# Routed expert stage: the scatter-add issued one tile later, four output buffers, expert weights split in pieces

## The reference

```python
x = x + L0_ffn(L0_cond(x, itok_B_1_198, cond0), ...)      # layer 0: dense FFN with top-2 LoRA experts
x = x + L1_ffn(L1_cond(x, itok_B_0_7, cond1, side), ...)  # layer 1: top-2 of 8 experts, and a shared one

# L1_ffn: t = 2048 tokens, d = 512, E = 8 experts, h = 352, K = 2
scores = softmax(x @ gate_w);  topk_w, topk_idx = top_k(scores, K)
comb = zeros((T, E)).at[arange(T)[:, None], topk_idx].add(topk_w)
g = silu(einsum('td,edh->teh', x, w_gate)) * einsum('td,edh->teh', x, w_up)
routed = einsum('teh,ehd,te->td', g, w_down, comb)
shared = silu(x @ sw_gate) * (x @ sw_up) @ sw_down
out = routed + shared
```

## Time and profile before

| | |
|---|---|
| median of 3 runs | 1144.67 us (1143.12 to 1146.67) |
| profiled execution | 1144.04 us, its span 1142.4 us |
| mean granted TensorE clock | 0.973 of full speed |
| TensorE matmuls busy | 1054.6 us, 92% |
| VectorE, ScalarE, GpSimd busy | 45%, 26%, 37% |
| GpSimd busy, 850 to 900 us | 38.99 of 50 us |
| chain that ended last: TensorE, VectorE, GpSimd, DMA | 76%, 7%, 5%, 5% |
| scatter-add, 39 of them | 1.60 us issue (median), 5.0 us to landing |
| gather, 39 of them | 1.00 us issue (median), 3.4 us to landing |

### The profile page before, as it was taken

One profiled execution on the slowest core, in us unless ns is written; L12 is line 12 of the kernel. 1 busy time (PEld: TensorE's weight loads), 2 busy tenths in 40 slices (PEclk: granted clock), 3 DMA queues, 4 the chain that ended last, 5 costly groups with the idle time before them and its releaser, 6 DMA issues.

```text
span 1142.4 us, 15264 instructions
## 1 busy us (share of the span) xinstructions
PE 1054.6 (92%) x4995; PEld 864.2 (76%) x4996; DVE 518.5 (45%) x776; ACT 299.0 (26%) x522; POOL 418.2 (37%) x403
## 2 busy tenths in 40 slices
PE   7847999999999999999979999999988889999995
PEld 4636888788878888788847777778777878889894
DVE  3395666644464445644475324362533224331400
ACT  1531222111111111111131110210034434444442
POOL 3663334440000000000025000027178778888984
PEclk9967999999999999999999999999999998999998
DMA  8723543444424434432337010500164554556442
GB/s 282 233 95 133 169 136 121 124 146 147 138 86 156 141 121 168 131 125 97 101 124 230 25 38 1 186 1 2 57 216 92 142 140 83 122 145 152 72 68 37
DMA packets 55706, 136.50 MB, mean 119 GB/s; under 512 B 11000, under 2 KB 12376, under 8 KB 55160
## 3 DMA queue, kind: packets, MB, share of 16 engines
q1 hardware_dynamic: 38952, 107.53, 27.9%
q0 software_dynamic: 13408, 25.61, 11.4%
q10 hardware_dynamic: 3312, 2.91, 0.9%
HBM read 96.89 MB, written 39.14 MB: 119 GB/s over the span
## 4 chain that ended last, share of the span: by engine, by line
PE 76%; DVE 7%; POOL 5%; DMA 5%; issue 4%; ACT 1%; SPq 0%; PEldq 0%; POOLq 0%; DVEq 0%; PEld 0%; ACTq 0%
PE ps_y L1385 5%; PE ps_y L1386 5%; PE ps_y L1387 5%; PE ps_h L1349 5%; PE ps_h L1351 5%; PE ps_h L1350 5%; DMA out_x<-yt,slot_tok 5%; PE ps_u L1392 3%; PE ps_u L1393 3%; POOL xg L691 2%; PE ps_y L1526 2%; PE ps_h L1511 2%; PE ps_y L1528 2%; PE ps_y L1527 2%; PE ps_h L1512 2%
## 5 line engine op out<-in xcount | busy, mean ns | idle before, releaser
L1027 DVE TENSOR_TENSOR h<-h,wb 128x512 f32<-128x512 f32 x64 | 44.2, 691 | 202.5 <-ACT h L813 202.5
L1385 PE MATMUL ps_y<-w_hi,g_hi 128*128 (+1 forms) x256 | 102.6, 401 | 16.9 <-DVE g_lo L1035 10.3
L810 ACT ACTIVATE h<-ps_h,bias 128x512 f32<-128x512 f32 x64 | 44.0, 688 | 243.1 <-PE ps_h L1359 242.8
L1386 PE MATMUL ps_y<-w_lo,g_hi 128*128 (+1 forms) x256 | 102.1, 399 | 0.0
L1387 PE MATMUL ps_y<-w_hi,g_lo 128*128 (+1 forms) x256 | 101.7, 397 | 0.0
L1349 PE MATMUL ps_h<-xt_hi,w_hl 128*128 128x512 f32 x256 | 100.0, 391 | 0.5 <-issue 0.5
L1351 PE MATMUL ps_h<-xt_hi,w_hl 128*128 128x512 f32 x256 | 99.7, 389 | 0.0
L1350 PE MATMUL ps_h<-xt_lo,w_hl 128*128 128x512 f32 x256 | 99.6, 389 | 0.0
L1201 DVE CAST eg_hi<-e_raw 128x2816 fp32r<-128x2816 f32 x8 | 14.3, 1789 | 160.4 <-PE ps_y L1614 149.4
L702 POOL DMA_INDIRECT out_x<-yt,slot_tok x39 | 73.6, 1888 | 31.0 <-DMA out_x<-yt,slot_tok 18.3
L683 POOL DMA_INDIRECT slot_d<-pay,pos_i x32 | 31.2, 975 | 142.9 <-DVE pay L1191 133.5
(11 more groups left out here) (273 smaller groups left out, 2601.0 us busy)
## 6 DMA issues: line engine op xcount, KB each, us to landing
w_hl<-w1s_d SPq DMA_DIRECT2D x49, 704.0 KB, 4.1
w1s_d<-w_hl SPq DMA_DIRECT2D x16, 704.0 KB, 4.7
e_raw<-in_wgu SPq DMA_DIRECT2D x8, 1408.0 KB, 7.9
w_raw<-in_w1b SPq DMA_DIRECT2D x16, 352.0 KB, 3.4
x_in<-in_x SPq DMA_DIRECT2D x4, 1024.0 KB, 7.0
xres<-in_x SPq DMA_DIRECT2D x16, 256.0 KB, 4.5
x_d<-xres SPq DMA_DIRECT2D x4, 1024.0 KB, 7.7
acc<-x_d SPq DMA_DIRECT2D x4, 1024.0 KB, 7.8
```

What stands on the lines that cost most here:

```text
L1027: tt(h1[u][:], h1[u][:], wb[:, v, :], ALU.mult).then_inc(gch, 1)
L1385: mm(ps_y[:, j, :], g_hi[u][:, cols], sl(w2_hi), start=first, **kw)
L1386: mm(ps_y[:, j, :], g_hi[u][:, cols], sl(w2_lo), start=False, **kw)
```

## The change

In the routed stage:

- GpSimd issues the scatter-add of tile t-1, not t, at the end of a tile's round: g_low(t), products(t+1), x_low(t+2), gather(t+5), scatter_add(t-1). The last one follows alone behind the loop.
- There are four `yt` buffers instead of two; the weighing of tile t waits for the landing of scatter-add t-4, not t-2. ScalarE's loop goes over four tiles instead of two.
- VectorE's split works chunk by chunk: the gate and up weights in 4 casts and 4 subtractions of 704 columns, the down weights in 3 and 3 of 512. Six instructions become 14; the data are the same.

```diff
-        yt = [sb(f"yt{u}", [P, D]) for u in range(2)]
+        yt = [sb(f"yt{u}", [P, D]) for u in range(4)]
...
-                pool.indirect_dma_start(out=out, in_=yt[t % 2][:], in_offset=None,
+                pool.indirect_dma_start(out=out, in_=yt[t % 4][:], in_offset=None,
...
-                scatter_add(t)
+                if t:
+                    scatter_add(t - 1)
+            scatter_add(SLOT_TILES - 1)
...
-            with act.Fori(1, SLOT_TILES // 2 - 1) as m:
-                for u in range(2):
-                    copies(m * 2 + u, u, (m * 2 + u - 1) * 16)
-            for t in range(SLOT_TILES - 3, SLOT_TILES):
-                copies(t, t % 2, (t - 1) * 16, t + 1 < SLOT_TILES, t + 2 < SLOT_TILES)
+            for t in range(4):
+                copies(t, t, None)
+            with act.Fori(1, (SLOT_TILES - 2) // 4) as m:
+                for n in range(4):
+                    copies(m * 4 + n, n, (m * 4 + n - 3) * 16)
+            for t in range((SLOT_TILES - 2) // 4 * 4, SLOT_TILES):
+                copies(t, t % 4, (t - 3) * 16, t + 1 < SLOT_TILES, t + 2 < SLOT_TILES)
...
                 if k == 0:
-                    nc.vector.tensor_copy(eg_hi[:, u], raw_g).then_inc(e_ch, 1)
+                    for c in range(DC):
+                        last = nc.vector.tensor_copy(eg_hi[:, u, c], raw_g[:, c])
+                    last.then_inc(e_ch, 1)
                 elif k == 1:
                     dve.wait_ge(e_ch, 2 * e + 1)
-                    tt(eg_lo[:, u], raw_g, eg_hi[:, u].bitcast(F32), ALU.subtract)
+                    for c in range(DC):
+                        tt(eg_lo[:, u, c], raw_g[:, c], eg_hi[:, u, c].bitcast(F32), ALU.subtract)
                 elif k == 2:
-                    nc.vector.tensor_copy(ed_hi[:, u, 0:full], raw_d)
+                    for c in range(full):
+                        nc.vector.tensor_copy(ed_hi[:, u, c], raw_d[:, c])
                     nc.vector.tensor_copy(ed_hi[0:tail, u, full], raw_t).then_inc(e_ch, 1)
                 else:
                     dve.wait_ge(e_ch, 2 * e + 2)
-                    tt(ed_lo[:, u, 0:full], raw_d, ed_hi[:, u, 0:full].bitcast(F32), ALU.subtract)
+                    for c in range(full):
+                        tt(ed_lo[:, u, c], raw_d[:, c], ed_hi[:, u, c].bitcast(F32), ALU.subtract)
```

More of the change, by code:

```diff
@@ L896, in g_high, with weigh @@
                 nc.scalar.copy(rgt_f[:], ps_u[:, 1, 0:HC * P]).then_inc(rgt_f_done, 1)
-            def weigh(t, u, stored):
+            def weigh(t, n, stored):
                 if stored is not None:
@@ L902, in weigh, with copies @@
                 act.wait_ge(ry_done, 1 + t + 1)
-                nc.scalar.activation(yt[u][:], ps_y[:, 2 + u, :], ACT.Copy, scale=slot_w[:, bass.ds(t, 1)])\
+                nc.scalar.activation(yt[n][:], ps_y[:, 2 + n % 2, :], ACT.Copy, scale=slot_w[:, bass.ds(t, 1)])\
                     .then_inc(ry_cp, 1)
-            def copies(t, u, stored, nxt=True, nxt2=True):
+            def copies(t, n, stored, nxt=True, nxt2=True):
+                u = n % 2
                 if nxt:
                     silu(t + 1, 1 - u)
-                g_high(t, first=stored is None and u == 0)
+                g_high(t, first=stored is None and n == 0)
                 if nxt:
@@ L913, in copies @@
                     x_high(t + 2)
-                weigh(t, u, stored)
+                weigh(t, n, stored)
             x_high(0, first=True)
@@ L919, in _ @@
             act.wait_ge(sy_done, NS * TPS)
-            copies(0, 0, None)
-            copies(1, 1, None)
-            with act.Fori(1, SLOT_TILES // 2 - 1) as m:
-                for u in range(2):
-                    copies(m * 2 + u, u, (m * 2 + u - 1) * 16)
-            for t in range(SLOT_TILES - 3, SLOT_TILES):
-                copies(t, t % 2, (t - 1) * 16, t + 1 < SLOT_TILES, t + 2 < SLOT_TILES)
+            for t in range(4):
[5 more added lines that the diff above has]
+                copies(t, t % 4, (t - 3) * 16, t + 1 < SLOT_TILES, t + 2 < SLOT_TILES)
         @block.vector
```

## The result

| | before | changed |
|---|---|---|
| median | 1145.01 us (1143.12 to 1146.67, 4 runs) | 1126.00 us (1123.57 to 1129.83, 4 runs) |
| ratio to before | | 0.9831, 95% interval 0.9800 to 0.9862 |
| profiled execution, its span | 1144.04, 1142.4 us | 1127.91, 1126.3 us |
| 36 tiles, weighing 0 to weighing 36 | 276.51 us | 252.52 us |
| from weighing 36 to the end of the span | 22.27 us | 26.90 us |

1.7% faster; 1129 with a range of 1117 to 1144 had been forecast. "Tail" is the last row of the table. "Body" is the loss without that of the first four tiles, the start: 35.5 - 6.5 = 29.0 before, 11.5 - 3.2 = 8.3 now.

The account below looks back on a forecast made before the run. TensorE sets the pace at 6.69 us a tile; 35.5 us are lost in the routed stage to late GpSimd. Terms -9.0 - 4.0 - 7.0 + 4.1 = -15.9 give 1128.1 profiled, 1129 as median, range 1117 to 1144.

Parts of the forecast that it names:

- Splits in pieces, -9.0: VectorE's split: GpSimd waits for shorter pieces, so each of six splits costs 0.5 us instead of 2.05, -9.0 us.
- The walk: Step along GpSimd's queue at a split: first L720 0.6 to 1.2 us late instead of 3.0, second about 1.7.
- The overrun rival: VectorE's split in 14 pieces outlasts the time until TensorE wants the next expert: about 1190 us; chance 0.04.
- The old price of 2.05: TensorE's loss in us per whole split, read from the last split, which has no load behind it.
- Start, -4.0: First four routed tiles: x_low waits less and the first round has no scatter-add, -4.0 of 6.5 us lost.
- Landing waits, -7.0: Scatter-adds waiting for their predecessor's landing behind five expert loads: 1.4 of 3.3 us off each, -7.0 us.
- Issued earlier against the load: Less late GpSimd issues the scatter-add some 1 us earlier relative to the expert load, which helps its landing.
- The rival without landing waits: The split ends some 3 us before the scatter-add, whose landing then needs 5 us: -26, 1119 us; chance 0.12.
- The move does nothing in the body: Scatter-add one tile later: same distance to its predecessor, and the weighing wait costs nothing in the body now.
- Tail, +4.1: Last scatter-adds, chained by landings of 5.46 us a step: the move leaves two steps after 36, +4.1 us.
- Slower through the tail: Pieces delay GpSimd as much as whole instructions, start gives 2.0, tail's 4.1 stands: +2.1, 1147 us; chance 0.13.
- the subtraction holds no DMA issue: VectorE's subtraction does not delay scatter-adds, so splits gain -5.4 us instead of -9.0, 1132 us; chance 0.04.

Follow-up runs that it names:

- the run without loads: Pieces alone (scatter-add in its own round, two buffers) without the weight loads of experts 2 to 7, against the kernel before: 1112.60 us, ratio 0.9715.
- experiment 9: The kernel before without the weight loads of experts 2 to 7, against the kernel before: 1130.76 against 1144.74 us, ratio 0.9868.
- experiments 9 and 10: Weight loads of experts 2 to 7 left out: 9 in the kernel before, 1130.76 us; 10 with the split in pieces, 1112.60; kernel before 1144.74.
- experiments 2 and 3: Against the kernel before: 2, the move with its four buffers, split whole, 1169.88 us, ratio 1.0014; 3, four buffers alone, 1169.47 us, ratio 1.0003.
- experiments 1 and 8: Against the kernel before: 1, the whole split in pieces and nothing else, 1139.54 us, ratio 0.9757; 8, only the subtractions in pieces, 1152.14 us, ratio 0.9866.
- experiment 1: The kernel before with only VectorE's split in pieces, two buffers and scatter-add in its own round: 1139.54 against 1168.73 us, ratio 0.9757.
- experiments 1 to 8: Two sets of follow-up runs; the kernel before takes 1168.73 us beside 1 to 4 and 1167.87 us beside 5 to 8.
- 9 to 12: Third set of follow-up runs, two without loads, one with loads held back, one with finer pieces; the kernel before takes 1144.74 us beside them.

## Why the prediction was right, and where it was off

- *What bounds.* Right: the pace is TensorE's, and what was lost was GpSimd's lateness. Loss went from 35.5 to 11.5 with TensorE's work unchanged.
- *Splits in pieces, -9.0.* The mechanism was right. A split now costs 0.5 us as forecast (6.70 + 7.14 in the first), also in the run without loads. The walk had L720 0.6 to 1.2 us late; the scatter-add ahead of it starts 878.70 - 871.60 - 6.69 = 0.4 us late and takes no longer than elsewhere. The split did not grow, 11.0 us against 11.8, when VectorE met gaps; 16 to 17 when it met few. The overrun rival had 18.7 as harmless, and so it was. The old price of 2.05 was too low. It was read from the last split alone, behind which the clock stays up. At 2.05 the term comes to -9.3; by experiment 9 the six splits had cost 17.7, and the term is -14.3.
- *The clock.* "Behind the 1.5 to 1.8 us stall of a split the clock mostly stays" was true of four of the six splits. Behind the other two it fell, and these are the two at 956.06 and 1019.64, the first of which has no landing wait at all and costs 5.7 us. The prediction had booked such costs under the landings. In the changed kernel the clock is 1.00 throughout, worth up to some 7.5 of the 24.0 us.
- *Start, -4.0.* -3.3 between the two profiled executions. But the pieces alone lose 4.6 or 0.5 us at the start from one execution to another, so the size is partly chance, and the two causes named, the shorter x_low and the first round without a scatter-add, were not separated.
- *Landing waits, -7.0.* With a split at 2.05 this term had to take the rest: 11.5 - 3.2 - 3.0 = 5.3 are left for five loads, 1.1 each where 1.9 was forecast, so -11.4. That overstates it. Only four of the five splits with a load have a landing wait behind them before the change (897.53, 929.94, 1009.11, 1040.44), and by experiments 9 and 10 the landings gave about 6.4, near the forecast. What carried it was not the sign that the prediction named, waits shrinking from 3.8 to about 2: there are still waits of 3.86 and 2.74. That a GpSimd which is less late absorbs more of each wait fits the rows (2.08 us at 900.80 cost 0.6) but was not tested by itself. "Issued earlier against the load" fits only some splits: a lead of 1.41 us let the next scatter-add pass without a wait, 0.75 gave 3.86. The rival without landing waits was half true, behind the splits at 947 and 975 us, where they are at most 1.25 us.
- *The move does nothing in the body.* Right, shown by experiments 2 and 3.
- *Tail, +4.1.* Right, 4.6 in the trace, 3.9 with the move alone, 4.4 beside the pieces alone.
- *Slower through the tail,* and *the subtraction holds no DMA issue:* both fell, by experiments 1 and 8.
- *The sum.* -15.9 forecast, -16.1 measured in the profiled execution. That it fits so closely is luck: the stage gave 4.0 us more than forecast (-24.0 against -20.0), the tail took 0.5 more, and 3.3 came from stages that the change does not touch. The medians differ by 19.0.

So the gain is the pieces' alone. They do better without the move: the change gives away some 4 us at its tail, and no run shows anything that the move earns in return.

## What to carry to other kernels

Where VectorE and GpSimd both work on SBUF, compare the longest instruction of the one with how late the other can be before the critical engine waits (here 3.09 us against some 1.2), and cut it to under that. Do not expect more from cutting further: the whole then takes longer, and what follows it moves. A short wait of TensorE can cost more than its length, if its clock falls behind it: price a stall from several of its occurrences, not from the cheapest. Look at which transfers whose landing is waited for leave just ahead of a big load; sending the load in parts that wait for each other made those waits shorter here, and it needs a load that is not due at once. A deferred DMA in a chain of landings was paid for once at the end of the chain, and issuing two in one round did not make it good.

## What was not expected of the hardware

- VectorE waits for a gap, and GpSimd seems not to: behind back-to-back GpSimd instructions a cast that takes 0.41 us alone took 4.36 us, and each of the changed kernel's last six splits took either 11.0 or 16 to 17 us; in the rows above GpSimd waited no longer than the VectorE instruction that was running.
- The same program takes 1145 us in one set of runs and 1168 in another, and nearly all of it is one place in an unchanged stage. The shared stage's down matmuls run from 644.2 to 826.1 us in the kernel before and from 643.4 to 850.0 in the pieces alone of experiment 1. In between, TensorE there nearly stops for some 25 us with work at hand (the windows view of the pieces alone, busy us (count) of each engine, granted clock, DMA share, GB/s):

```profile
770.00:780.00 10.00, 10.00 (x46) 8.29 (x45) 1.33 (x2) 0.00 (x0) 7.56 (x9) 1.00 0.03 3
...
790.00:800.00 10.00, 2.62 (x5) 1.33 (x5) 0.00 (x0) 0.00 (x0) 7.56 (x9) 0.50 0.02 1
```

Five matmuls start in 10 us instead of 46, at 1.2 GHz, and no engine's wait ends before them in the record. It is there, between 780 and 810 us, in every execution that was profiled for experiments 1 to 8, and in none of the others. Whether it goes with the chip is not shown: the record gives experiments 1 to 4 and 9 to 12 the same chip number, and 5 to 8 another. The cause stays open. The kernel before of each set was run beside it, so the ratios compare like with like.
